# Four attention layers and four expert layers on one core: row maxima and scores computed on two halves of TensorE's rows

## The reference, cut to what matters

```python
# layer 0: 16 heads of 8 channels, 4 batches ... regrouped as 8 units, 256 queries x 256 keys per head
q = (Wq @ x + bq).reshape(B, 16, 8, T) ; k, v alike
p = softmax(q^T k / sqrt(8))
# layer 3: 16 heads of 16 channels, 1024 queries x 1024 keys per head
q = fq_sym(q * scale)   # s = max|q| / 127 per token and head; q = round(q / s) * s
k = fq_sym(k) ; v = fq_sym(v, axis=tokens)
p = softmax(q k^T)
p = round(p / (max(p) / 255)) * (max(p) / 255)
out = p @ v
```

## Time and profile before

| | us |
|---|---|
| median of 3 runs | 1283.31 (1281.79 to 1284.55) |
| profiled execution, device time | 1287.61 |
| its span, first to last instruction | 1285.7 |
| start, before the first maxima of layer 0 | 0 to 33 |
| layer 0's attention | 33 to 221 |
| layer 3's attention, unit 0's maxima | about 814 to 849 |
| layer 3's attention, the rest | about 849 to 1100 |

### The profile page before, as it was taken

The page is one execution under the profiler, slowest core; times in us unless marked ns, Lnnn a source line. Parts: engine busy times, 40 slices in busy tenths (PEclk is TensorE's granted clock), DMA queues, the critical chain, the costliest instruction groups (busy, mean ns, idle before and its releaser), DMA issues.

```text
span 1285.7 us, 18945 instructions
## 1 busy us (share of the span) xinstructions
PE 969.9 (75%) x6616; PEld 574.1 (45%) x6616; DVE 650.2 (51%) x1546; ACT 439.9 (34%) x720; POOL 383.9 (30%) x527
## 2 busy tenths in 40 slices
PE   1868787688448889677637981698989999469993
PEld 1434444577314435455424761234444544336662
DVE  1757663335258723256764335787878783301111
ACT  1335545211015521144410430045655667112210
POOL 3213210211375200333304006135555557110002
PEclk9989989688759989878858995569989999679997
DMA  8643641365454200455432663201031000620002
GB/s 191 137 98 90 171 104 62 145 205 170 150 130 123 64 25 0 131 84 98 82 131 77 199 183 94 45 1 38 2 104 35 2 2 2 268 88 25 17 13 74
DMA packets 117820, 117.64 MB, mean 91 GB/s; under 512 B 71848, under 2 KB 107240, under 8 KB 114408
## 3 DMA queue, kind: packets, MB, share of 16 engines
q1 hardware_dynamic: 106496, 95.58, 27.3%
q10 hardware_dynamic: 8160, 12.46, 3.4%
q0 software_dynamic: 3072, 8.39, 2.2%
HBM read 90.53 MB, written 29.62 MB: 93 GB/s over the span
## 4 chain that ended last, share of the span: by engine, by line
PE 48%; DVE 14%; POOL 6%; issue 6%; DMA 4%; ACT 3%; SPq 0%; POOLq 0%; ACTq 0%; DVEq 0%
PE psT L1392 6%; PE psT L1093 6%; PE psB L1093 5%; PE psT L1244 5%; PE psB L1210 4%; PE psO L1288 3%; DVE mxp L1770 3%; PE psB L1406 3%; PE psT L1355 2%; PE psB L1433 2%; PE psB L1457 2%; PE psO L1278 2%; PE psB L1101 1%; POOL scr_sorted L2161 1%; DVE mxp L1774 1%
## 5 line engine op out<-in xcount | busy, mean ns | idle before, releaser
L1770 DVE TENSOR_REDUCE mxp<-psB 128x1 f32<-128x512 f32 x256 | 162.4, 685 | 41.6 <-PE psB L1210 40.5
L1244 PE MATMUL psT<-whole 99*128 99x256 bf16 (+2 forms) x1024 | 156.9, 279 | 11.3 <-issue 10.9
L1774 DVE TENSOR_REDUCE mxp<-psB 128x2 f32<-128x512 f32 x192 | 122.6, 685 | 52.5 <-PE psB L1216 52.4
L1216 PE MATMUL psB<-whole 96*128 96x256 bf16 x384 | 77.8, 315 | 64.3 <-issue 55.0
L1244 PEld LDWEIGHTS psT<-whole 99*128 99x128 bf16 (+2 forms) x1024 | 98.5, 103 | 60.8 <-issue 27.8
L1545 ACT ACTIVATE Pt<-psT,ln 128x1024 f32<-128x1024 f32 x96 | 106.6, 1114 | 54.9 <-PE psT L1244 53.8
L1545 ACT ACTIVATE Pt<-psT 128x1024 f32<-128x1024 f32 x96 | 97.9, 1023 | 73.2 <-PE psT L1244 71.5
L2096 POOL TENSOR_TENSOR rstd<-vare,cst 128x1 f32<-128x1 f32 x64 | 35.6, 559 | 277.8 <-DVE vare L1694 277.6
L1210 PE MATMUL psB<-whole 96*128 96x512 bf16 x256 | 96.6, 434 | 4.2 <-DVE mxp L1770 3.0
L1216 PEld LDWEIGHTS psB<-whole 96*128 96x128 bf16 x384 | 31.4, 107 | 114.2 <-issue 84.4
L1392 PE MATMUL psT<-whole,qf 128*128 x176 | 81.4, 606 | 0.6 <-ACT qf L1594 0.6
(11 more groups left out here) (300 smaller groups left out, 1793.7 us busy)
## 6 DMA issues: line engine op xcount, KB each, us to landing
whole<-in_w SPq DMA_DIRECT2D x32, 512.0 KB, 4.9
whole<-in_w SPq DMA_DIRECT2D x5, 3072.0 KB, 10.2
xn<-scr_sorted ACTq DMA_DIRECT2D x42, 128.0 KB, 2.2
scr_q<-sq SPq DMA_DIRECT2D x48, 96.0 KB, 1.9
scr_k<-sk SPq DMA_DIRECT2D x48, 96.0 KB, 1.9
whole<-scr_k SPq DMA_DIRECT2D x24, 192.0 KB, 3.5
whole<-scr_k SPq DMA_DIRECT2D x72, 64.0 KB, 3.8
whole<-scr_q SPq DMA_DIRECT2D x64, 64.0 KB
```

What stands on the lines that cost most here:

```text
L1216: ins = pe.matmul(dst[:, i * 256:(i + 1) * 256], lhsT=q_at[:, h * A.T + s.tc * P:h * A.T + (s.tc + 1) * P], rhs=k_at[:, h * A.T:(h + 1) * ...
L1244: ins = pe.matmul(psT[:, s.n % 2, i * A.T:(i + 1) * A.T], lhsT=k_at[:, h * kw + s.c * P:h * kw + (s.c + 1) * P], rhs=q_at[:, h * A.T:(h + ...
L1770: dve.tensor_reduce(mxp[:, s.un.g % 2, at:at + 1], psB[:, s.n % BANKS, :], AX.X, ALU.max).then_inc(bank_used[s.n % BANKS], 1)
L1774: dve.tensor_reduce(mxp[:, s.un.g % 2, at:at + 2], psB[:, s.n % BANKS, :].rearrange("p (h n) -> p h n", h=2), AX.X, ALU.max).then_inc(bank ...
```

## The change

In layer 3, the maxima no longer come from the float32-accurate six products. Quantised q is an integer between -127 and 127 times a step. The integers, taken before they are multiplied back (`ints_made`), are transposed by PE (`fit`, two new steps a unit), copied by ACT as bfloat16, stored and loaded by SP (`ints`: 1 DMA, `ints_packs`: 6 DMAs a unit) onto rows 0 to 47 and 64 to 111 of a tile of their own (words 0 to 6143 of `whole` for units 0 to 2, `ctx_t` for unit 3). They meet the three parts of k, which now lie on rows 0 to 47 and 64 to 111 as well. A maxima step is now a pair: keys 0 to 511 on rows 0 to 47 into one bank, keys 512 to 1023 on rows 64 to 111 into another; both banks must be free before the first matmul. `negsplit` multiplies the maximum by the step (`kept`), one more small DVE operation. The scores proper get a seventh product (112 rows, 115 with the maxima). `w12load` moves from unit 1 to the end of unit 2's maxima.

In layer 0, even heads lie on rows 0 to 47 and odd heads on rows 64 to 111, maxima rows at 48 and 112. The zeros are no longer loaded. Maxima steps are pairs too (four matmuls into two banks), and `st` alternates between the halves, each half writing its own bank of `psT`. q and k need 6 pack DMAs each instead of 3, in elements of 512 bytes, the maxima 4 DMAs instead of 2, the ones 6 instead of 3.

```diff
+K3_ROWS = ((0, 0, 3), (48, 0, 1), (64, 0, 3))
+Q3_ROWS = ((0, 0, 3), (48, 2, 1), (64, 1, 2), (96, 1, 1))
-    dict(front=0.077, fronts=[0.0, 0.01, 0.02, 0.03, 0.04, 0.058, 0.06, 0.079], store=0.294, packs=0.3, max=1.011, max_end=1.919, neg=2.006, body=1.639, end=3.415, start=0, span=1.008, max_first=1.026)]
+    dict(front=0.077, fronts=[0.0, 0.01, 0.02, 0.03, 0.04, 0.05, 0.054, 0.058, 0.06, 0.079], ints=0.2, ints_packs=0.21, store=0.294, packs=0.3, max=1.011, max_end=1.919, neg=2.006, body=1.639, end=3.415, start=0, span=1.008, max_first=1.026)]
-                out += [fq3(j) for j in range(A.nb)] + [q3, fqt(0), fqt(1), split]
+                out += [fq3(j) for j in range(A.nb)] + [q3, fit(0), fit(1), fqt(0), fqt(1), split]
-            if A.layer == 3 and u == 1:
-                streams += [([lambda: add("w12load", s=last["td"])], u + at["body"] + 0.5, u + at["body"] + 0.5)]
+            if A.layer == 3 and u == 2:
+                streams += [([lambda: add("w12load", s=units[2].last_S)], u + at["max_end"] + 0.05, u + at["max_end"] + 0.05)]
...
+                elif s.kind == "ints":
+                    u = s.un
+                    for m in u.m_ints:
+                        turn(sp, bank_used, m)
...
+                    sp.dma_start(di[u.g % 2].rearrange("(m p) n -> p m n", m=2), ints_of(u.g)).then_inc(ints_stored[u.g % 2], 16)
+                elif s.kind == "ints_packs":
...
+                    for r in (0, 64):
+                        for c in range(3):
+                            at = r + 16 * c
+                            sp.dma_start(QI(u.u)[at:at + 16, :].rearrange("d (h n) -> d h n", h=16),
+                                         di[u.g % 2].rearrange("(d h) n -> d h n", d=16)).then_inc(ints_packed[u.g % 2], 16)
...
+                elif s.kind == "fit":
+                    dst = m_begin(s.m)
+                    pe.wait_ge(ints_made, s.i + 1)
+                    for j in range(s.un.A.nb):
+                        ins = pe.transpose(dst[:, j * P:(j + 1) * P], tmp[:, j * 256 + s.c * P:j * 256 + (s.c + 1) * P], ident)
+                    ins.then_inc(bank_ready[s.m % BANKS], 1)
...
                     free(pe, bank_used, s.n)
+                    if A.layer == 0:
+                        free(pe, bank_used, s.n2)
+                        for tc in range(2):
+                            for odd, n in ((0, s.n), (1, s.n2)):
+                                r, at = 64 * odd, s.j * 256
+                                ins = pe.matmul(psB[:, n % BANKS, tc * 256:(tc + 1) * 256],
+                                                lhsT=QP[r:r + 48, u.g % 3, at + tc * P:at + (tc + 1) * P],
+                                                rhs=kslot(A, u)[r:r + 48, at:at + 256], start=True, stop=True)
+                                if tc == 1:
+                                    ins.then_inc(bank_ready[n % BANKS], 1)
+                    elif A.layer == 3:
+                        free(pe, bank_used, s.n2)
+                        for r, n in ((0, s.n), (64, s.n2)):
+                            keys = s.j * NT + (512 if r else 0)
+                            ins = pe.matmul(psB[:, n % BANKS, :],
+                                            lhsT=QI(u.u)[r:r + 48, s.j * A.T + s.tc * P:s.j * A.T + (s.tc + 1) * P],
+                                            rhs=KP[r:r + 48, keys:keys + 512], start=True, stop=True)
+                            ins.then_inc(bank_ready[n % BANKS], 1)
...
+                        if A.layer == 0:
+                            r, at, to = 64 * (i % 2), (h // 2) * 256, place(A, i) * 256
+                            ins = pe.matmul(psT[:, s.n % 2, to:to + 256],
+                                            lhsT=kslot(A, u)[r:r + 50, at + s.c * P:at + (s.c + 1) * P],
+                                            rhs=QP[r:r + 50, u.g % 3, at:at + 256], start=True, stop=True)
+                            continue
...
-            for i in range(3):
-                for at in (2048 * i, 6144 + 2048 * i):
-                    act.dma_start(arena[48:96, at:at + 2048], t["zeros"][0:384, :].rearrange("(p k) n -> p (k n)", k=8)
-                                  ).then_inc(zeroed[i], 16)
...
+                elif s.kind == "fit":
...
+                    act.activation(ints_of(u.g)[:, s.c, :], m_slot(s.m), ACT.Copy).then_inc(bank_used[s.m % BANKS], 1)
...
+                link(dve.tensor_scalar(src, dst, MAGIC, MAGIC, ALU.add, ALU.subtract))
+                dve.sem_inc(ints_made, 1)
...
+        def QI(u):
+
+            return w0[:, 2048 * u:2048 * (u + 1)].bitcast(BF16) if u < 3 else \
+                ctx_t[:, :, :].rearrange("p k n -> p (k n)").bitcast(BF16)
...
+                        step = kept[:, s.un.g % 2, :].rearrange("p (t h) -> p t h", t=A.TC)[:, :, s.j * HP:(s.j + 1) * HP]
+                        link(dve.tensor_tensor(mx.rearrange("p (t h) -> p t h", t=A.TC),
+                                               mx.rearrange("p (t h) -> p t h", t=A.TC), step, ALU.mult))
...
+def pack3(sp, dst, src, width, sem, blocks, h0, h1):
+
+    for at, c0, n in blocks:
+        sp.dma_start(dst[at:at + n * 16, :].rearrange("r (h n) -> r h n", h=16)[:, h0:h1, :],
+                     src[c0:c0 + n, :, 0:width].rearrange("c (d h) n -> (c d) h n", d=16)[:, h0:h1, :]).then_inc(sem, 16)
...
+        if A.layer == 0:
+            for odd in range(2):
+                r = 64 * odd + at * 8
+                sp.dma_start(dst[r:r + n * 8, 0:2048].rearrange("r (j n) -> r j n", j=8),
+                             src[c0:c0 + n, :, 0:width].rearrange("c (d j t) n -> (c d) j t n", d=8, t=2)[:, :, odd, :]
+                             ).then_inc(sem, 16)
+            at += n
+            continue
```

More of the change, by code:

```diff
@@ L247, in front @@
             r.packed_before = packed[r.g % 2]
[L248 removed]
+            packed[r.g % 2] += 16 * (6, 6, 3, len(Q3_ROWS))[A.layer]
             r.packed = packed[r.g % 2]
@@ L291, in fqt, with fit, f @@
                 return f
+            def fit(m):
+                def f():
+                    s = add("fit", un=r, c=m, i=r.i, m=take("M"))
+                    r.m_ints = (r.m_ints or []) + [s.m]
+                return f
             def split():
@@ L313, in maxes @@
             r.neg = []
-            per = A.H * A.NC * P // 512 // A.parts
+            per = {0: A.H // 2, 1: A.H * A.NC * P // 512, 3: A.H}[A.layer] // A.parts
             for part in range(A.parts):
                 tiles = []
-                for tc in range(A.TC):
+                for tc in range(1 if A.layer == 0 else A.TC):
                     for j in range(part * per, (part + 1) * per):
                         def f(tc=tc, j=j):
-                            r.last_S = add("smax", A=A, un=r, tc=tc, j=j, first=(tc == 0 and j == 0), n=take("S")).n
+                            s = add("smax", A=A, un=r, tc=tc, j=j, first=(tc == 0 and j == 0), n=take("S"))
+                            s.n2 = take("S") if A.layer != 1 else None
+                            r.last_S = s.n if A.layer == 1 else s.n2
                         tiles.append(f)
@@ L590, in sorted_pairs @@
                 add("k3load", i=K3_AT.index(t), m=shared)
-        last["td"] = tiles[TILES2 - 1].s
         def gather(b):
@@ L797, in flamingo @@
         dk = [nc.dram_tensor(f"scr_k{i}", [3, 2 * P, 256], BF16).ap() for i in range(2)]
+        di = [nc.dram_tensor(f"scr_i{i}", [2 * P, 256], BF16).ap() for i in range(2)]
         dk3 = nc.dram_tensor("scr_k3", [3, 2 * P, NT], BF16).ap()
@@ L817, in flamingo @@
         v_set = sem("v_set")
-        zeroed = [sem(f"zeroed{i}") for i in range(3)]
         bias_made, x_biased = sem("bias_made"), sem("x_biased")
@@ L850, in flamingo @@
         quant_q = sem("quant_q")
+        ints_made = sem("ints_made")
+        ints_stored, ints_packed = pair("ints_stored"), pair("ints_packed")
         v_quant = sem("v_quant")
@@ L911, in m_slot, with place @@
             return psB[:, n % BANKS, 0:256]
+        def place(A, i):
+            return i % 2 * 2 + i // 2 if A.layer == 0 else i
         def evacuated(eng, n):
@@ L954, in _ @@
                     A = s.A
-                    if A.has_max:
+                    if A.layer == 0:
+                        for r in range(3):
+                            for at in (48, 112):
+                                sp.dma_start(KP[at:at + 2, 4096 * r:4096 * r + 2048], t["ones3"][0:2, 0:2048]).then_inc(k_ones, 16)
+                    elif A.has_max:
                         for r in range(4 if A.layer == 3 else 3):
@@ L1200, in _ @@
                     A, u, K = s.A, s.un, s.A.rows
-                    if s.first:
+                    if s.first and A.layer == 3:
+                        pe.wait_ge(ints_packed[u.g % 2], 96 * (u.u // 2 + 1))
+                        pe.wait_ge(k3_in, 48 * len(K3_AT))
+                    elif s.first:
                         wait_packs(pe, s)
-                        if A.layer == 0 and u.u < 3:
```

(8 more changed lines are left out.)

78 lines of the change are left out of this document (54 added, 24 removed).

## The result

The changed kernel is slower: 1304.42 us median (1302.97 to 1312.25, 4 runs) against 1283.93 (1281.79 to 1290.41, 4 runs) on the same chip; ratio 1.016, 95% interval 1.012 to 1.020. Its profiled execution has a span of 1301.1 us where the kernel before has 1285.7.

The account below looks back on a forecast made before the run. Layer 3 was taken as TensorE's, layer 0 as a latency chain, the first 33 us as DMAs only. Layer 3's -2.1 and layer 0's -15.3 took 1287.6 to 1270.2, or 1266 against the median; range 1253 to 1285.

Parts of the forecast that it names:

- Layer 3, step 1 (maxima in slots, -10.9): Layer 3's slots: 91 pairs stream 0.22 instead of 0.44 us, less 0.10 for one more shape change: -10.9 us.
- C: Rival: row halves take turns instead of running together; layer 3 at +18, total +6, 1289 us; chance 0.10.
- Step 2 (alone, +4.3): Layer 3's unit 0, maxima alone: a pair needs both banks, 1.40 instead of 1.20 us, 21 pairs: +4.3 us.
- Step 3 (fronts, +3.5): Layer 3's fronts: second `fqt` starts about 1.2 us later behind a maxima pair's reductions, three times: +3.5 us.
- Step 4 (the rest, +1): Layer 3's small extra operations, copies and DMAs, and `w12load` some 50 us later but in time: +1 us.
- Layer 0, step 1 (start, -5.5): Layer 0's start: without the zeros' loads the packs go out at about 18.5 to 19.5 us: -5.5 us.
- Step 3 (chain, -7.4): Layer 0's chain, first pack issue to first maxima: 8.69 as in layer 1 against 9.75, 7 units: -7.4 us.
- Rival E: Packs no faster, SP's 12 issues and small elements eat the gain; PE stalls in slots: total -5, 1278 us; chance 0.10.
- Step 4 (clock, +1.5): Layer 0 between first maxima and next projection: the clock falls after each longer idle wait, costing +1.5 us.
- rival D: Layer 0: less PE work keeps the clock lower through more of each unit; total -7, 1276 us; chance 0.08.
- (5): Sign in layer 0: first pack issue to first maxima 8.7 instead of 9.75 us, PE's idle before it above 2.32.
- rival B: Layer 3: a pair's two weight loads or a drain stand open, +0.1 a slot; total -8, 1275 us; chance 0.12.

Follow-up runs that it names:

- x4: Changed kernel, but in both layers a pair's first matmul waits only for its own bank, the second for the other: 1294.23 us, ratio 1.0069.
- x3: Changed kernel with the 3 MB load of w12 issued about half a unit later: 1301.09 us, ratio 1.0121.
- y1: Changed kernel with the edits of x3 and x4 together: 1292.05 us, ratio 1.0054.
- y3: Kernel before, 96 rows, with DVE writing layer 0's zeros instead of six DMAs: 1275.55 us, ratio 0.9945.
- y2: y1 with layer 0's even and odd heads stored apart, so its twelve packs move 4096 bytes at a time: 1271.13 us, ratio 0.9896.
- x8: Kernel before with layer 0's six packs issued as twelve with 512-byte elements: 1297.65 us, ratio 1.0126.
- z3: Kernel before with twelve packs a unit in layer 0, split at head 8, elements of 4096 bytes: ratio 0.9952.
- x6: Changed kernel, but in layer 0 one half's matmuls are issued one behind the other, so halves hardly overlap: 1308.22 us, ratio 1.0208.
- x5: Kernel before with layer 0 on 48 rows (50 in the scores) instead of 96, zeros left out, no halves: 1345.68 us, ratio 1.0487.
- x7: Changed kernel, but in layer 3 both matmuls of a maxima pair use rows 0 to 47: 1373.5 us, ratio 1.0676.

## Why the prediction was wrong

I forecast 1266 and faster with 0.76. It came out slower, on a side to which I gave 0.17, and for other reasons than the rival there.

**Layer 3, step 1 (maxima in slots, -10.9).** The mechanism and the size in a slot were right: 1.52 against 1.51, so the halves run together and C falls, and a change of shape costs what I took. What failed is the count, "182 are left, 91 pairs". Slot by slot, before against after, 43 of the 91 are some 0.11 shorter (4.8 us); 23 more, away from handovers and fronts, come out even. And I had taken the handovers out of the sum as ruled by DVE and given them no price of their own. The three took 26.0 us instead of 22.2 (+3.8), the slot ahead of each 2.94 instead of 2.43 (+1.5), and the four or five slots behind each 7.7 us more in all, at the lower clock: the fourth slot behind each handover takes 3.1 to 3.3 us instead of 1.9, of which the record has 2.7 to 3.3 at the lower level. That is +13.0 where the sum had nothing.

**Step 2 (alone, +4.3).** Right in kind: 1.45 a pair against my 1.40. Unit 0's stretch grew by 5.9, from 32.7 to 38.6, and x4 shows the cause, the claim on both banks, by taking 4.9 of it away.

**Step 3 (fronts, +3.5).** The mechanism is there, the cost is not. The second `fqt` does wait for a pair's reduction, timeline in unit 2's front against the earlier trace rows:

```profile
881.55 0.69 DVE L1862 TENSOR_REDUCE mxp<-psB 128x1 f32<-128x512 f32 x1
...
882.16 0.68 DVE L1865 TENSOR_REDUCE mxp<-psB 128x1 f32<-128x512 f32 x1
882.30 0.29 PEld L1199 LDWEIGHTS psB<-cst,tmp 128*128 128x128 f32 x2 [0.32 <-DVE mxp L1862]
...
882.89 0.29 PEld L1199 LDWEIGHTS psB<-cst,tmp 128*128 128x128 f32 x2 [0.31 <-DVE mxp L1865]
```

But this front's three slots took 3.80 + 7.42 + 2.37 instead of 3.37 + 6.83 + 2.62, +0.8, and the four slots of unit 3's front took 16.0 instead of 16.6; with the slot ahead of each the two fronts cost 0.6 together. Unit 1's front lies in unit 0's maxima and has no price of its own.

**Step 4 (the rest, +1).** This step failed outright: "`w12load` some 50 us later, still 100 us ahead of the last experts". I asked when the load is needed and not what it stands in front of. It costs 5 us (x3; slot by slot, a wait of 4.4 and 1.5 for the lower clock behind it). I had named it among what would make me wrong.

Layer 3 in all: forecast -2.1, measured +20.0. Slot by slot it is +5.9 in unit 0, +13.0 at the handovers, +5.9 at the wait for the maxima's rows, +0.6 in the fronts and -5.5 in all other slots. x4 and x3 take 17 of it away (y1); 3 stay: +0.8 in unit 0, +3.6 in the handovers (24.6 us) and the slots ahead of them, +3.1 behind the last handover, the only one that the lower clock still follows, +1.7 in the fronts, -0.1 at the wait, -6.1 in all other slots. Why the clock falls behind one handover and not behind another stays open.

**Layer 0, step 1 (start, -5.5).** Right: 28.41 against 32.83, -4.4, and y3 gets the same by another way, so the zeros were the cause. With large elements it is -7.8, so the small packs ate 3.4 of it. But the gain in the first maxima didn't reach the first scores (51.2 against 51.8 us), as the twelve packs of the next unit stand before the maxima's rows; with large elements (y2) the first scores run at 42.7.

**Step 3 (chain, -7.4).** This is the step that turned layer 0's sign. I took layer 1's 8.69 us with small elements against layer 0's 9.75 with large ones, and put the difference down to the elements. In layer 1 nothing ran beside it; in layer 0 PE worked on slots for most of the 9.75 and idled for 2.32, so the two numbers didn't measure the same thing. The row that did was in plain sight: SP's own time, three large packs in 1.16 us against six small ones in 3.02, 0.39 and 0.50 each, and 0.72 in the changed kernel. x8 prices the step at +12 in the stretch and +2.4 at the start, z3 the number alone at -4. Rival E had the place right ("12 issues of SP ... and the small elements eat the gain"), and a price of 0 for it.

**Step 4 (clock, +1.5).** Far too small. I held that it comes back soon after each wait, from 0.92 over layer 0, and argued against rival D with it; the record has 85 us at the lower level in place of 32. x6 shows that it isn't from the overlap, and x5 that fewer rows alone keep TensorE at 1.2 GHz while it is busy all the time. What these 85 us cost in time no run here measures by itself. And the 0.92 was itself too high: up to 53 us it stood for no record, and six matmuls in 1.44 us are 1.2 GHz.

**Step 2** and the terms -2 of step 4 and -3.5 of step 5 lie within the noise of the stretches and were not told apart. Layer 0's stretch and start in all: forecast -15.3, measured +5.3.

Of my signs, (1) to (4) and (6) came, within 0.05 us a pair and 0.4 us at the start; (5) failed: 11.7 from the first issue to the first maxima, not 8.7, and no idle time of PE before it; PE worked on slots at the lower clock meanwhile.

The Trainium skill, TensorEngine Tiling (Array Packing), Key Properties, says that a change of the tiling mode drains TensorE. The changed kernel changes shape once more in each slot, and the slot is at 1.52; with a drain in it, as priced in rival B, it would be at 1.60. By this the trace shows none of that size.

## What to carry to other kernels

When a DMA is cut into more and smaller pieces, price it by the queue's own issue time at that element size, and look at what stands behind it in the queue; a layout in DRAM that keeps elements at 4096 bytes, and nothing else, turned 1.0054 into 0.9896 (y1 to y2). When an operation takes two buffers of a ring of three, let each part wait for its own. A stretch that is taken out of a sum because another engine rules it still needs a price: the handovers, left out here, cost 13 us. A load that is moved must be checked against the small transfers that it will stand before, not only against its own deadline.

## What the runs showed of the hardware that was not expected

- The clock can stay low with no idle TensorE, when matmuls use 48 rows. x5 (48 to 50 rows) stayed at 1.2 GHz for 176.62 busy of 178 us; x7 (48 rows, one half at a time) stayed at 0.50 with PE busy 23.00 of 23 us, 27 us in all after a handover. With two halves at once the same fall lasted 6.8 us.
- The clock column shows 1.00 ahead of the record's first entry (53 us before, 301 us in x5), whatever TensorE runs at; the distance of two matmuls tells.
- SP needs 0.72 us to issue a pack of layer 0 with elements of 512 bytes (x8), 0.37 with 4096 (y2) and 0.39 with 8192 bytes. In layer 1 a pack with 512 bytes takes 0.50, so the element isn't all that counts.
- DVE zeroes 96 x 2048 float32 in 1.76 us, six times over within its idle time, where the DMAs that zeroed 48 rows needed 11.8 us to land.
